# Column halves for one product and another order of scatters in a linear-attention and expert kernel

## The reference, cut to what matters

```
A = einsum('bhntd,bhnsd->bhnts', q, k) * decay      # "probabilities", lower triangle only
o_intra = einsum('bhnts,bhnsd->bhntd', A, v)
o_int   = einsum('bhtd,bhde->bhte', q * exp(gc), S)  # the part of the carried state S
S = exp(gt) * S + einsum('bhtd,bhte->bhde', k * exp(gt - gc), v)
o = (o_intra + o_int), normed per head, times g * sigmoid(g), then @ Wo
```

## Time and profile before

| what | value |
|---|---|
| median of 3 runs | 447.07 us (446.12 to 447.21) |
| the profiled execution's own time | 444.98 us |
| its span (first to last instruction) | 443.3 us |
| PE busy | 419.6 us, 95% |
| POOL, ACT, DVE busy | 287.4, 310.6, 308.5 us |

### The profile page before, as it was taken

The page is one execution under the profiler, slowest core; times in us unless marked ns, Lnnn a source line. Parts: engine busy times, 40 slices in busy tenths (PEclk is TensorE's granted clock), DMA queues, the critical chain, the costliest instruction groups (busy, mean ns, idle before and its releaser), DMA issues.

```text
span 443.3 us, 12400 instructions
## 1 busy us (share of the span) xinstructions
PE 419.6 (95%) x3074; PEld 366.9 (83%) x3075; DVE 308.5 (70%) x930; ACT 310.6 (70%) x952; POOL 287.4 (65%) x245
## 2 busy tenths in 40 slices
PE   8997999999999999999999999989999999999990
PEld 6665788888778877877877888889999999999990
DVE  5985798897756757657667567866766776866760
ACT  3688888687867867767678678746666766666660
POOL 8530253456776776767767763417888888888884
PEclk9999899999999999999999999999999999999996
DMA  9725378336456343454454444004554555555540
GB/s 239 190 83 170 140 235 302 139 116 163 134 145 175 91 130 114 120 154 154 134 160 134 117 132 134 12 29 72 70 68 63 71 62 65 69 66 64 74 37 0
DMA packets 59096, 51.29 MB, mean 116 GB/s; under 512 B 7200, under 2 KB 51392, under 8 KB 59072
## 3 DMA queue, kind: packets, MB, share of 16 engines
q1 hardware_dynamic: 45936, 42.07, 34.0%
q0 software_dynamic: 12272, 8.54, 14.0%
q10 hardware_dynamic: 864, 0.40, 0.4%
HBM read 33.14 MB, written 18.30 MB: 116 GB/s over the span
## 4 chain that ended last, share of the span: by engine, by line
PE 63%; ACT 14%; POOL 5%; issue 5%; another core or an unknown queue 5%; DVE 4%; ACTq 1%; DVEq 0%; POOLq 0%
PE psA L905 14%; PE psVG L893 14%; ACT E L1069 8%; PE psO L746 7%; PE psVG L716 5%; POOL rms L544 4%; PE psA L729 4%; PE psQK L704 3%; PE psO L631 2%; PE psO L759 2%; DVE ms L1384 2%; PE psT L770 2%; PE psT L778 2%; ACT sq L1078 2%
## 5 line engine op out<-in xcount | busy, mean ns | idle before, releaser
L578 POOL DMA_INDIRECT out_dram<-yw,sidx x71 | 114.9, 1618 | 29.0 <-issue 9.1
L544 POOL TENSOR_TENSOR rms<-msn,neg_half 128x8 f32<-128x8 f32 x32 | 53.2, 1661 | 42.8 <-DVE msn L1388 42.8
L1069 ACT ACTIVATE E<-gcB,ngc 128x128 f32<-128x128 f32 x256 | 78.5, 400 | 0.0
L746 PEld LDWEIGHTS psO<-v_sb,pr 128*128 128x128 f32 x512 | 64.6, 191 | 14.7 <-issue 12.0
L746 PE MATMUL psO<-v_sb,pr 128*128 128x64 f32 x512 | 66.5, 273 | 8.5 <-DVE og L1428 4.7
L550 POOL DMA_INDIRECT sorted_rows<-x_all,pos_i x64 | 63.3, 989 | 17.1 <-issue 17.1
L537 POOL TENSOR_SCALAR_AFFINE_SELECT E<-E 128x1024 f32<-128x1024 f32 x32 | 35.5, 1111 | 51.5 <-ACT E L1069 51.0
L1384 DVE TENSOR_REDUCE ms<-sq 128x8 f32<-128x512 f32 x32 | 21.9, 686 | 62.1 <-ACT sq L1078 62.0
L1078 ACT ACTIVATE sq<-psO 128x512 f32<-128x512 f32 x32 | 19.1, 596 | 41.9 <-remote 40.0
L1416 DVE TENSOR_TENSOR pr<-psA,E 128x512 f32<-128x512 f32 x64 | 40.9, 680 | 0.0
L905 PE MATMUL psA<-xT_all,v_sb 128*128 x288 | 38.2, 276 | 0.4 <-issue 0.4
(11 more groups left out here) (191 smaller groups left out, 957.2 us busy)
## 6 DMA issues: line engine op xcount, KB each, us to landing
gcB<-decay_rows SPq DMA_DIRECT2D x32, 512.0 KB
sorted_rows<-blank SPq DMA_DIRECT2D x12, 396.0 KB, 5.6
xg<-sorted_rows SPq DMA_DIRECT2D x71, 66.0 KB
x_all<-in_L_attn_x_dram SPq DMA_DIRECT2D x16, 256.0 KB, 5.3
out_dram<-res SPq DMA_DIRECT2D x32, 128.0 KB
eqB<-decay_exp_rows SPq DMA_DIRECT2D x32, 64.0 KB
w1b<-in_L_ffn_w_dram SPq DMA_DIRECT2D x8, 256.0 KB
xT_all<-in_L_ffn_w_dram SPq DMA_DIRECT2D x32, 64.0 KB
```

Of the source, the lines that this page charges most:

```text
L544: nc.gpsimd.tensor_tensor(rms[:], msn[:], neg_half[:, 0:2 * H], ALU.pow).then_inc(rms_ready, 1)
L578: nc.gpsimd.indirect_dma_start(out=out_rows, out_offset=bass.IndirectOffsetOnAxis(ap=sidx[j][:], axis=0), in_=yw[j][:], in_offset=None, bo ...
L746: last = nc.tensor.matmul(psO[:, k * HV + h * DV:k * HV + (h + 1) * DV], pr[:, h // 2, k * SEQ + h % 2 * P:k * SEQ + (h % 2 + 1) * P], v_s ...
L1069: last = nc.scalar.activation(E[j][:, k, h * P:(h + 1) * P], gcB[j][:, k * H + h, :], ACT.Exp, bias=ngcf[:, bass.ds((s * 2 + k) * H + h, 1)])
```

## The change

Two edits are made together.

The first is in `own_half` and `outputs`. Each product into `psO` is split in two: output rows 0 to 63 (which need weight columns 0 to 63, and use the left half of the array) and rows 64 to 127 (the right half). Each call loads 64 columns of weights and streams the same values, so `outputs` now has 8 calls, 2 with the state, and 8 again, instead of 4, 1 and 4.

```
                 for h in range(H):
-                    last = nc.tensor.matmul(psO[:, k * HV + h * DV:k * HV + (h + 1) * DV], pr[:, h // 2, k * SEQ + h % 2 * P:k * SEQ + (h % 2 + 1) * P],
-                                            v_sb[j][:, k, h * DV:(h + 1) * DV], ...)
+                    for c in range(2):
+                        t = k * SEQ + h % 2 * P + c * P // 2
+                        last = nc.tensor.matmul(psO[c * P // 2:(c + 1) * P // 2, k * HV + h * DV:k * HV + (h + 1) * DV], pr[:, h // 2, t:t + P // 2],
+                                                v_sb[j][:, k, h * DV:(h + 1) * DV], ...)
...
-                nc.tensor.matmul(psO[:, HV:2 * HV], qe[j][:], S_sb[:], start=False, stop=False, skip_group_check=True)
+                for c in range(2):
+                    nc.tensor.matmul(psO[c * P // 2:(c + 1) * P // 2, HV:2 * HV], qe[j][:, c * P // 2:(c + 1) * P // 2], S_sb[:],
+                                     start=False, stop=False, skip_group_check=True)
```

```
             def step(s):
+                t = (s - PLACE_FROM) * 3
                 if s < SEQS:
                     mask_dec(*divmod(s, 2))
+                if s == PLACE_FROM:
+                    pool.wait_ge(dve_late, LATE)
+                    pool.wait_ge(sort_cleared, CLEARS * 16)
+                if s >= PLACE_FROM and t < TILES:
+                    pool.wait_ge(qk_ready, s + 2)
+                    place_rows(t)
                 if s >= 1:
                     if s >= 2:
                         pool.wait_ge(dve_on, s - 1)
                     rms_step(*divmod(s - 1, 2))
...
-                if s >= PLACE_FROM:
-                    place_rows(s - PLACE_FROM)
+                if s >= PLACE_FROM and t + 1 < TILES:
+                    place_rows(t + 1)
+                    pool.wait_ge(oT_ps_ready, s)
+                    place_rows(t + 2)
```

More of the change, by code:

```diff
@@ L544, in rms_step, with place_rows @@
                 nc.gpsimd.tensor_tensor(rms[:], msn[:], neg_half[:, 0:2 * H], ALU.pow).then_inc(rms_ready, 1)
-            def place_rows(s):
-                pool.sem_inc(tick, 1)
-                for t in range(s * 3, min(s * 3 + 3, TILES)):
+            def place_rows(t):
+                if t < TILES:
+                    pool.sem_inc(tick, 1)
                     nc.gpsimd.indirect_dma_start(out=sorted_dram, out_offset=bass.IndirectOffsetOnAxis(ap=pos_i[:, t:t + 1], axis=0),
@@ L561, in step @@
                     finish_band()
-                if s == PLACE_FROM:
-                    pool.wait_ge(dve_late, LATE)
-                    pool.wait_ge(sort_cleared, CLEARS * 16)
-                if s >= PLACE_FROM:
-                    place_rows(s - PLACE_FROM)
+                if s >= PLACE_FROM and t + 1 < TILES:
+                    place_rows(t + 1)
+                    pool.wait_ge(oT_ps_ready, s)
+                    place_rows(t + 2)
             for s in range(SEQS + 1):
@@ L745, in own_half @@
                 for h in range(H):
-                    last = nc.tensor.matmul(psO[:, k * HV + h * DV:k * HV + (h + 1) * DV], pr[:, h // 2, k * SEQ + h % 2 * P:k * SEQ + (h % 2 + 1) * P],
-                                            v_sb[j][:, k, h * DV:(h + 1) * DV], start=(k == 0 and h == 0), stop=(k == 1 and h == H - 1),
-                                            skip_group_check=True)
+                    for c in range(2):
+                        t = k * SEQ + h % 2 * P + c * P // 2
+                        last = nc.tensor.matmul(psO[c * P // 2:(c + 1) * P // 2, k * HV + h * DV:k * HV + (h + 1) * DV], pr[:, h // 2, t:t + P // 2],
+                                                v_sb[j][:, k, h * DV:(h + 1) * DV], start=(k == 0 and h == 0), stop=(k == 1 and h == H - 1),
+                                                skip_group_check=True)
                 return last
```

## The result

The changed kernel takes 437.03 us (median of 4 runs, 436.84 to 437.41); the kernel before took 447.14 beside it (446.12 to 448.22). The ratio is 0.9751, with an interval of 0.9716 to 0.9786: 10 us faster. The prediction was 419 us. The direction is right and the time lies in the range, but only a good third of the forecast gain came.

The account below looks back on a forecast made before the run. TensorE was taken to bound short steps, its report held back by scatters the long ones; 23.3 us from 21 scatter steps plus 5.0 from nine others, 28.3 together, gave 419 us (own range 413 to 427, with rivals 411 to 441).

Parts of the forecast that it names:

- The halves: In `outputs`, column halves load and multiply side by side, 0.056 us a pair: 1.59 us, 0.58 less.
- The short step: Attention steps without scatters fall from 7.40 us to 6.85 (bounds 6.8 and 7.0), 5.0 us over nine.
- B: In `outputs`, matmuls pair but loads don't: 0.30 us more than now, 441 us in all; chance 0.12.
- C: In `outputs`, column halves take turns: 0.81 us more per step, 456 us in all; chance 0.14.
- D: In `outputs`, no load runs beside the other half's matmul: 2.7 us more, 513 us in all; chance 0.03.
- The held report: In scatter steps, scatters hold back TensorE's report on `outputs`; with it prompt, 21 x 0.71 = 14.9 us go.
- What is late next: In scatter steps, TensorE, GpSimd and ScalarE lie within 0.3 us: 7.0 us a step (bounds 6.8 and 7.4).
- the power's cover: On GpSimd, the power and `on` come 1.2 us later, hidden until after `outputs`; about 1 us of cover stays.
- sign of a power moved too far back: At TensorE's transposes: if `on` becomes what they wait for, the power stands too late; no size given.
- the 0.6 us of room: Behind the third scatter, mask, probabilities and `og` still finish before `outputs` is due, about 0.6 us to spare.
- A: In scatter steps, halves pair but a moved scatter holds another report: steps 7.4 us, 427 us in all; chance 0.16.
- E: In `outputs` and the scatters, halves are neutral and reports stay held as long: 447 us; chance 0.03.

Follow-up runs that it names:

- e5: Changed kernel with its first scatter back behind the power, so two stand in a row and the third waits for the transposes: 443.99 us; 443.07 in session 4.
- e2: Kernel before with only GpSimd's new order of scatters, products of full width as before: 443.95 us, ratio 0.9912.
- e3: Changed kernel with VectorE's residual moved ahead of `on` and `qe` from step 6 on: 424.96 us, ratio 0.9491 to the kernel before.
- f4: Changed kernel with the residual first and the third scatter waiting for `o_ready` instead of the transposes' report, run in session 3: 421.20 us, ratio 0.9402.
- f3: Changed kernel without the third scatter's wait for the transposes' report, run in session 3: 435.52 us, ratio 0.9714.
- e4: Changed kernel without the third scatter's wait for the transposes' report, run in session 2: 435.85 us, ratio 1.0099 to the kernel before.

## Why the prediction was right and wrong

**The halves: right.** Pairs were forecast at 0.056 us and `outputs` at 1.59; it takes 1.51. The short step came at 6.89 us for 6.85. Rivals B, C and D are out. The Trainium skill (TensorEngine Tiling (Array Packing), Key Properties) has tiles load and multiply in parallel; the trace now agrees for column halves, with 16 passes in 0.51 us. The Trainium skill (TensorE: Matmul & The Clock Gate, The mechanism) has the rule that a load overlaps only products of another row group; the same 16 passes disagree with it. Rival D, which was priced for that case, has a slip in its sum: 0.245 x 64 / 256 is 0.061 and not 0.053, which makes D some 522 us instead of 513. Nothing hangs on it, since D is out.

**The held report: right, and of the size stated.** It is gone in the changed kernel in every session. The term was 21 x 0.71 = 14.9 us; the kernel before, in the one session without holds, takes 431.3 us, 14.6 to 17.3 less than in the three others (445.9 to 448.6). Of its cause the prediction said only that such scatters hold it back. The traces narrow this down. In the 14 traces of sessions with holds (that of the result among them) 144 `outputs` ended while a scatter that followed directly on another one was the last thing GpSimd had begun; each of their reports was held, by 0.38 to 2.77 us. Another 157 ended behind a scatter that stood alone or was the first of its row, or in the mask after them, and none of these was held by more than 0.24. The orders differ in where `outputs` falls: behind the second or third of a row in before and e5 (but for the last step, which has one scatter), never so in the change, e2, e3 and f4, and in f3 only in the step shown above. So it isn't the scatter ahead of the power as such. That this place is the cause, and not something that goes with it, no run tested.

**What is late next: here it failed.** The step that failed is "I take 7.0 us for steps with scatters (bounds 6.8 and 7.4)". The measured step is 7.83, beyond the upper bound. Its reason failed with it, that three engines near 6.8 us only add some friction. They form a loop. Three things in it were not priced:

- The residual. The prediction counted the power's cover up to `outputs` ("about 1 us stays") and let TensorE's transposes wait for `on`. They wait for the residual too, which stands behind `qe`, 0.6 us more. This was to be read in the order on VectorE, and e3 shows its price: 12 us. The prediction's own sign of a power moved too far back, that the transposes wait for `on`, did show (16.2 us).
- The start of a waiting scatter. "The mask then ends about 1.0 + 1.1 = 2.1 us after that report" leaves out 0.81 us between the transposes' end and the scatter. It is 2.9 us, which uses up the 0.6 us of room, and TensorE waits 0.16 for `og`.
- The wait on the transposes was priced as what is queued behind it, and not followed round to itself: what it waits for itself waits for the power, which stands behind it.

**The sum.** In the profiles, forecast and measured: short steps 5.0 us for nine; measured 2.1 for the four steps from 61.34 us (the same start in both) to the first row and its counterpart 90.06, and 0.51 for each later one. Scatter steps 23.3; measured 177.64 - 173.08 = 4.6. This term alone explains the miss: 20 steps are 0.83 us too long and the first two, at 8.2, 1.2 each, together 19. The spans differ by 443.3 - 435.7 = 7.6 us. The medians differ by 10.1, as the profiled execution of before lay 2.1 us below its median and that of the change 0.4 above.

**The rivals.** A named another report held back, with steps of 7.4; the view of waits of the changed kernel has no wait behind an unnamed engine. E fell with the halves. The real case was none of them: the wait put in against the hold closed a loop. Its time, 437, lies between A (427) and B (441). That it lies in the range at all is luck: the slow end was there for B, in which the loads don't pair, and they do. The slower side had a case that nobody named: in a session without holds the kernel before takes 431.3, and 437 would be slower. The changed kernel itself wasn't run in such a session; its variant e4 was 1.0% slower there, and has the same time with holds and without (435.5 and 435.9).

**Parts and whole.** Against before in session 1 the halves alone cost 1.4 us and the scatters alone give 4.0; the two together gave 10.1, 11.4 and 8.4 in the sessions with holds. Each part waits for a wall of its own: the halves behind the held report, the scatters behind a loop that has `outputs` in it. Between e2 and the changed kernel, 7 us apart, 3.1 us lie in six steps without scatters and 2.3 in the 22 with them, where the residual's loop, almost as long as the one that the halves shorten, takes over; the other 1.4 lie in the start.

## What to carry to other kernels

When a change adds a wait, follow what is waited for back through every engine until it reaches something that nothing in this step holds up; if the walk comes back to the waiting instruction, its length is a lower bound for the step, whatever the busiest engine needs. There can be several such loops, and a gain ends at the next longest (here 7.83, 7.24, and TensorE's own 6.89). Of what an instruction waits for, list also who must empty its output buffer, and where that stands in its engine's order: one instruction moved ahead of two others gave 12 us, where the whole change gave 10. And measure the kernel before again in every session: its own time moved by 15 us on one chip, more than the change is worth.

## What the runs showed of the hardware

- The hold on TensorE's reports beside GpSimd's indirect transfers (up to 2.0 us in before, up to 2.8 with the halves alone, and there pauses of TensorE of up to 1.5 too) is neither the program's nor the chip's alone: the same program on chip 5 had none in one session (431.2 us) and one in every scatter step of another (442.2). Within a session the times of before, 12 to 19 runs, stay within 1.2% and never cross from one kind to the other. In the sessions with holds a report was held when its product ended behind a scatter that followed directly on another (144 of 144, 0.38 to 2.77 us) and not otherwise (157 of 157, at most 0.24); without holds, 22 such reports in session 2 were prompt (at most 0.02). What it belongs to stays open.
- A scatter that waits for a semaphore starts 0.8 us after the report (0.81 behind the transposes, 0.82 behind `qk_ready` in e4); one that finds its wait fulfilled starts 0.2 to 0.3 us after the work ahead of it.
- The scatter behind the power takes 1.50 us in every order with another one ahead of the power, but 1.03 in the second scatter step of each, and 1.03 (1.19 the first time) in all orders without one ahead, with holds or without. No run tells why.
- VectorE's scaling `msn` of 128 x 8 numbers takes 0.17 us alone and up to 1.80 beside GpSimd's mask and scatters (e2; mean 0.62 in the changed kernel, 0.17 before). Its nine long ones in the changed kernel, of 1.76 to 1.77, end within 0.08 us of the mask's end.
